# A graph transformer on one core: q fetched two quads in front, one bank for the maxima

## The chip, the cores and the metric

The kernel runs on one core of one Trainium2 chip. The metric is the device time of the whole program in microseconds, the median of the runs. Three runs of the kernel before gave 4218.53, 4223.54 and 4201.57 us.

## The reference

The model is a graph transformer with two layers on 6250 nodes of 128 features and 100000 edges that are sorted by their target node, followed by a projection, a residual and a normalisation. There are 32 edge types, 16 node types and 8 heads of 16. One layer, cut to what matters here:

```python
q = typed_linear(x, ntype, Wq)                    # per node
kT = einsum('nhd,htdo->nhto', k, Watt)            # per node and edge type
vT = einsum('nhd,htdo->nhto', v, Wmsg)
kw, m = kT[src, :, etype], vT[src, :, etype]      # one row per edge
a = einsum('ehd,ehd->eh', kw, q[dst]) * pri / SQRT_D
att = edge_softmax(a, dst, n)                     # segment max, exp, sum, per target
hag = segment_sum(m * att, dst)                   # per target node
h = layernorm(silu(typed_linear(hag, ntype, Wa)) * alpha + x * (1 - alpha))
```

## The kernel before, in words

Each layer has two stages. The first (`fused`) computes k, v and q of the nodes and writes a table to memory: for each source node and edge type one row of 256 floats, 128 of the key and 128 of the message. The second (`attend`), the stage that the change touches, goes over the edges.

The edges lie in slots: 26 blocks of 32 tiles, a tile of 128 edges whose targets lie in one tile of 128 nodes. Four tiles make a quad, so a block has 8 quads and a layer 208. The order of work is written out by hand: each engine has its own program, a loop over blocks with the 8 quads (q = 0 to 7) written out, six blocks in a turn of the hardware loop. Engines wait for one another by semaphores that count quads. What each does in its step t:

- POOL (L795) gathers the table rows of the edges of a quad into `rows` by four indirect DMAs of 128 rows of 1 KB. `rows` holds three blocks. Quad t+11 may be gathered when quad t-13 has been summed; in the first three blocks POOL is held by `q_psum` instead, ten quads ahead (`LEAD`).
- DVE builds the turned one-hot matrix of a quad (`turned`, L1752): it compares the edges' places in the node tile, loaded by SP into a ring of four, with the row number. A matrix has 128 x 512 floats and lies in `region_q` behind the q of all nodes. There are two places.
- PE fetches q of each edge by matmuls of this matrix with the q of the node tile (`fetch_q`, L1270), four matmuls (eight records in the profile) into bank 1 or 2. It does this for quad t+1.
- DVE multiplies the gathered keys by q from the bank (`multiply`, L1744), sums over each head (`head_sums`, L1757), and later weighs messages by the exponentials (`weigh`, L1766, quad t-12).
- PE sums the weighted messages and weights per node (`sum_quad`, L1283, quad t-13) with one-hot matrices that ACT builds (L1014, L1017), and DVE adds the four results to `sums` (`add`, L1781, quad t-14).
- The maxima of the block before are found by a chain that is spread over the steps q = 0 to 5 (`find_maxima`): DVE masks the scores, PE turns them (L1313, q = 0, bank 3), DVE scans (L1812, L1815), PE brings the chunk ends into a row (L1321, q = 1, bank 4), DVE carries them on (L1822 and below), PE turns them back (L1327, q = 2, bank 4), DVE adds them (L1838 to L1844), PE turns the maxima (L1334, q = 3, bank 3), DVE subtracts them (L1850), ACT takes the exponentials. In q = 5 PE spreads the factor of a node whose edges cross the block border (L1297, bank 4).

In a step PE has the order: crossing (q = 5), sum, fetch, chain step. DVE has the order: multiply, crossing (q = 6), then four places, each with one addition; behind the addition of place 0 the one-hot matrix of quad t+2, of place 1 the head sums, of place 3 the weighing; and behind these the chain's step of that place. The waits of the fetch and of its matrix are

```python
pe.wait_ge(onehotT_ready, quad + 1)
wait(pe, prod_ready, quad - 1)         # the multiplication that used the bank last
...
wait(dve, q_psum, quad - 1)            # the fetch that used the matrix's place last
```

At the end of the second layer POOL stores the sums by indirect DMAs (L805) while the last quads are still at work.

## Time and profile before

| | us |
|---|---|
| runs: median, lowest, highest | 4218.53, 4201.57, 4223.54 |
| profiled execution: span | 4190.3 |
| of that, attention of layer 0 (641 to 2010) | 1369 |
| of that, attention of layer 1 (2621 to 4010) | 1389 |
| DVE busy | 2714.8 (65%) |
| POOL busy | 2540.4 (61%) |
| PE busy | 2425.6 (58%) |
| ACT busy | 1707.4 (41%) |

The page gives the profiled execution a span, from the first to the last instruction, and no further time. Busy times are of the whole span. In the two attention stages the traffic is about 110 to 120 GB/s, in the stages that write the table about 400 GB/s. "Idle before" is the time in which an instruction's engine did nothing just before it, and the name behind it is what ended that. Ends of matmuls are modelled, not measured. "Remote" means that the view knows no instruction of this core that ended the wait.

### The profile page before, as it was taken

The numbers are of one execution on the slowest core, as the hardware profiler recorded it, in microseconds if no ns is written. First come the engines' busy times: TensorE is split into PE (matmuls) and PEld (weight loads), VectorE is DVE, ScalarE is ACT, GpSimd is POOL, SyncE is SP. The second block draws the span as 40 slices with busy tenths as digits, with TensorE's granted clock in tenths as the row PEclk, the third lists the DMA queues.
The fourth block names the chain that finished last, engine by engine and source line by source line (L and its number), as shares of the span: only waits on it lengthen the run. The fifth ranks groups of instructions, "written<-read, shape, count | busy, mean of one in ns | idle before, by whom it ended". The sixth has DMA issues, their size and how long they took to land.

```text
span 4190.3 us, 54460 instructions
## 1 busy us (share of the span) xinstructions
PE 2425.6 (58%) x12785; PEld 1767.6 (42%) x12786; DVE 2714.8 (65%) x6706; ACT 1707.4 (41%) x3970; POOL 2540.4 (61%) x2596
## 2 busy tenths in 40 slices
PE   3777771455555556556677777145555555555355
PEld 2333331355445555455333333144544444444343
DVE  7666662566666666667778877156766667666465
ACT  3666660233223333324566666022333333223255
POOL 4666556666666666661566664666666666666426
PEclk8899885677777777776799888577777777777666
DMA  8999984344444444444799997444444444444131
GB/s 202 406 412 409 417 356 136 110 118 123 123 117 117 120 119 120 116 115 109 249 382 375 409 390 326 131 114 117 116 114 113 113 113 112 114 113 114 51 112 48
DMA packets 321826, 782.64 MB, mean 187 GB/s; under 512 B 87083, under 2 KB 249803, under 8 KB 309007
## 3 DMA queue, kind: packets, MB, share of 16 engines
q0 software_dynamic: 110672, 651.37, 44.2%
q1 hardware_dynamic: 202387, 127.10, 11.7%
q8 instruction: 126, 2.06, 0.2%
q10 hardware_dynamic: 8448, 0.53, 0.1%
q14 instruction: 193, 1.58, 0.1%
HBM read 335.58 MB, written 573.46 MB: 217 GB/s over the span
## 4 chain that ended last, share of the span: by engine, by line
DVE 19%; issue 19%; PE 18%; DMA 16%; another core or an unknown queue 16%; ACT 5%; DVEq 4%; POOL 3%; SPq 0%; POOLq 0%; ACTq 0%
DMA relation_table<-region,scatter_node 14%; PE bank L1283 6%; DVE sums L1781 6%; PE bank L1270 4%; PE bank L1116 3%; ACT region L878 3%; DVE region L1766 2%; DVEq L1770 1%; DVE region L1744 1%; DVEq L1781 1%; DVE region_q L1752 1%; PE bank L1146 1%; PE bank L1321 1%; DVEq L396 1%
## 5 line engine op out<-in xcount | busy, mean ns | idle before, releaser
L795 POOL DMA_INDIRECT region<-relation_table,key_of x1664 | 1634.6, 982 | 886.5 <-issue 461.9
L1283 PE MATMUL bank<-region,arena 128*128 128x136 f32 x3328 | 694.3, 371 | 514.5 <-DVE region L1766 298.4
L1014 ACT ACTIVATE arena<-iota_free,minus_dst 128x128 f32<-128x128 f32 x1664 | 528.4, 388 | 831.7 <-remote 433.9
L1283 PEld LDWEIGHTS bank<-region,arena 128*128 128x128 f32 x3328 | 600.6, 262 | 594.6 <-DVE sums L1781 290.0
L1744 DVE TENSOR_TENSOR region<-bank,region 128x512 f32<-128x512 f32 x416 | 285.1, 685 | 871.2 <-remote 670.3
L1116 PE MATMUL bank<-sums,arena 128*128 128x512 bf16 x2048 | 630.7, 418 | 244.0 <-ACT region L878 212.2
L878 ACT COPY region<-bank 128x512 f32<-128x512 f32 x1152 | 624.4, 601 | 359.9 <-DMA relation_table<-region,scatter_node 220.9
L1570 DVE COPY region<-bank 128x512 f32<-128x512 f32 x896 | 585.5, 685 | 264.7 <-DMA relation_table<-region,scatter_node 173.5
L1270 PE MATMUL bank<-region_q 128*128 x3328 | 604.5, 342 | 187.9 <-issue 99.4
L1270 PEld LDWEIGHTS bank<-region_q 128*128 128x128 f32 x3328 | 570.8, 257 | 201.7 <-issue 201.2
L1781 DVE TENSOR_TENSOR sums<-sums,bank 128x136 f32 x1664 | 473.6, 285 | 78.7 <-DVE sums L1781 29.9
L1025 ACT ACTIVATE region<-arena 128x256 f32<-128x256 f32 x52 | 21.7, 417 | 1031.4 <-DVE arena L1850 789.2
L1116 PEld LDWEIGHTS bank<-sums,arena 128*128 128x128 bf16 x2048 | 197.0, 103 | 577.1 <-ACT region L878 295.8
L1766 DVE TENSOR_TENSOR region<-region 128x512 f32<-128x512 f32 x416 | 284.0, 683 | 2.1
L1757 DVE TENSOR_REDUCE arena<-region 128x32 f32<-128x512 f32 x416 | 280.4, 674 | 0.1
L1017 ACT ACTIVATE arena<-arena 128x512 f32<-128x512 f32 x416 | 262.0, 630 | 13.1
L718 POOL TENSOR_TENSOR sums<-arena,sums 128x256 f32<-128x256 f32 x128 | 86.1, 673 | 266.2 <-ACT arena L896 262.7
L1752 DVE TENSOR_SCALAR region_q<-arena,row_no 128x512 f32<-128x512 bf16 x416 | 206.9, 497 | 13.8 <-issue 7.3
L1577 DVE COPY arena<-bank 128x1024 bf16<-128x1024 bf16 x256 | 175.4, 685 | 49.9 <-issue 14.1
L1137 PE MATMUL bank<-identb,sums 128*128 128x128 bf16 x2048 | 176.2, 236 | 4.1 <-POOL sums L722 4.1
L1137 PEld LDWEIGHTS bank<-identb,sums 128*128 128x128 bf16 x2048 | 152.9, 107 | 58.5 <-issue 18.4
L735 POOL DMA_INDIRECT relation_table<-region,scatter_node x128 | 128.9, 1007 | 73.6 <-issue 33.3
(243 smaller groups left out, 2655.3 us busy)
## 6 DMA issues: line engine op xcount, KB each, us to landing
arena<-edge_places SPq DMA_DIRECT2D x416, 128.0 KB
region<-relation_table,key_of POOLq DMA_INDIRECT x1664
arena<-segment_flags SPq DMA_DIRECT2D x104, 128.0 KB
region_q<-q_rows SPq DMA_DIRECT2D x6, 768.0 KB, 6.5
aggregated_rows<-one_less_alpha SPq DMA_DIRECT2D x17, 256.0 KB
region<-aggregated_rows SPq DMA_DIRECT2D x16, 272.0 KB, 3.0
sums<-relation_weight_parts SPq DMA_DIRECT2D x32, 128.0 KB
x_sorted<-arena SPq DMA_DIRECT2D x16, 256.0 KB
```

The costliest lines, as they stand in the source:

```text
L795: pool.indirect_dma_start(out=rows[:, block_.r, q * QUAD + s], out_offset=None, in_=table, in_offset=bass.IndirectOffsetOnAxis(ap=key_of[: ...
L878: nc.scalar.copy(stage[:, r, :, k * HS:(k + 1) * HS], bank[TABLE_BANK + k % TABLE_BANKS][:, :].rearrange("p (t o) -> p t o", t=RT)).then_i ...
L1014: chain.step(nc.scalar.activation(onehots[:, at, s], iota_free[:, :], ACT.Abs, bias=minus_dst[:, bass.ds(block_.b * BLOCK + (q * QUAD + s) ...
L1116: nc.tensor.matmul(bank[TABLE_BANK + k % TABLE_BANKS][:, :], x_spreadT[:, k, :], w_rel[:, k, :], start=True, stop=True).then_inc(table_psu ...
L1137: ins = nc.tensor.transpose(bank[SPREAD_BANK[half]][:, :].bitcast(BF16)[:, k * P:(k + 1) * P], x_spread[:, tile.par, half * H + k].rearran ...
L1270: ins = nc.tensor.matmul(bank[1 + q % 2][:, s * D:(s + 1) * D], onehotT[:, q % 2, s], q_rows[:, bass.ds(tiles[s], 1), :].rearrange("p a n ...
L1283: ins = nc.tensor.matmul(bank[SUM_BANK[q % 2][pair]][:, s * SUMC:(s + 1) * SUMC], onehots[:, at, 2 * pair + s], rows[:, block_.r, slot, RH ...
L1570: v.tensor_copy(stage[:, r, :, k * HS:(k + 1) * HS], bank[TABLE_BANK + k % TABLE_BANKS][:, :].rearrange("p (t o) -> p t o", t=RT)).then_in ...
L1744: v.tensor_tensor(here, bank[1 + q % 2][:, :].rearrange("p (s d) -> p s d", s=QUAD), here, ALU.mult).then_inc(prod_ready, 1)
L1757: v.tensor_reduce(score[:, block_.par, q * QUAD:(q + 1) * QUAD, :], rows[:, block_.r, q * QUAD:(q + 1) * QUAD, 0:D].rearrange("p s (h o) - ...
L1766: v.tensor_tensor(msg, msg, bc(part[:, :, RHS0:D], 3, HS), ALU.mult).then_inc(weighted, 1)
L1781: v.tensor_tensor(total, total, bank[SUM_BANK[q % 2][n // 2]][:, (n % 2) * SUMC:(n % 2 + 1) * SUMC], ALU.add).then_inc(sum_added, 1)
```

## The change

q is fetched for quad t+2 in PE's step t, and its one-hot matrix is built for quad t+3 in DVE's step t. The q lies in banks 1, 2 and 4 in turn, the matrices in three places, and all five steps of the maxima on PE use bank 3. The place of a quad is its number in the layer modulo 3. In front of the first step PE fetches two quads instead of one, and DVE builds three matrices instead of two.

```diff
+Q_BANK = (1, 2, 4)
+Q_AHEAD = len(Q_BANK) - 1
+CHAIN_BANK = 3
...
-        onehotT = wqf[:, NTILES * D:NTILES * D + 2 * QUAD * P].rearrange("p (r s e) -> p r s e", r=2, s=QUAD)
+        onehotT = wqf[:, NTILES * D:NTILES * D + len(Q_BANK) * QUAD * P].rearrange("p (r s e) -> p r s e", r=len(Q_BANK), s=QUAD)
...
+        def q_place(block_, q):
+
+            return (block_.at * QPB + q) % len(Q_BANK)
+
...
                     pe.wait_ge(onehotT_ready, quad + 1)
-                    wait(pe, prod_ready, quad - 1)
+                    wait(pe, prod_ready, quad - Q_AHEAD)
+                    at = q_place(block_, q)
                     for s in range(QUAD):
-                        ins = nc.tensor.matmul(bank[1 + q % 2][:, s * D:(s + 1) * D], onehotT[:, q % 2, s],
+                        ins = nc.tensor.matmul(bank[Q_BANK[at]][:, s * D:(s + 1) * D], onehotT[:, at, s],
...
                         if q % 2 == 0:
-                            tiles = slot_tiles(block_.b, q + 1)
-                        coming = ahead(block_, q, 1)
+                            tiles = slot_tiles(block_.b, q + Q_AHEAD)
+                        coming = ahead(block_, q, Q_AHEAD)
...
-                fetch_q(Block(0, 0), 0, slot_tiles(0, 0))
+                tiles = slot_tiles(0, 0)
+                for q in range(Q_AHEAD):
+                    fetch_q(Block(0, 0), q, tiles[QUAD * q:])
...
-                    v.tensor_tensor(here, bank[1 + q % 2][:, :].rearrange("p (s d) -> p s d", s=QUAD), here, ALU.mult).then_inc(prod_ready, 1)
+                    v.tensor_tensor(here, bank[Q_BANK[q_place(block_, q)]][:, :].rearrange("p (s d) -> p s d", s=QUAD), here, ALU.mult).then_inc(prod_ready, 1)
...
-                    wait(dve, q_psum, quad - 1)
-                    flat = onehotT[:, q % 2].rearrange("p s e -> p (s e)")
+                    wait(dve, q_psum, quad - Q_AHEAD)
+                    flat = onehotT[:, q_place(block_, q)].rearrange("p s e -> p (s e)")
...
-                        coming = ahead(block_, q, 2)
+                        coming = ahead(block_, q, Q_AHEAD + 1)
...
-                for q in range(2):
+                for q in range(Q_AHEAD + 1):
                     turned(Block(0, 0), q)
```

Everywhere else `bank[3]` and `bank[4]` of the chain (L1297, L1313, L1321, L1327, L1334 on PE and their readers on DVE) become `bank[CHAIN_BANK]`.

## Rows read from the trace of the kernel before

**Rows 1.** Windows, attention stages: stretch, length, busy us by engine, clock, DMA share, GB/s.
```profile
641.00:2010.00 1369.00, 733.65 (x3818) 644.70 (x3819) 849.83 (x2321) 405.91 (x1104) 826.45 (x843) 0.71 0.44 118
2621.00:4010.00 1389.00, 702.81 (x3796) 611.82 (x3796) 834.75 (x2288) 402.20 (x1093) 858.89 (x874) 0.72 0.39 108
```

**Rows 2.** The chain that ended last, shares of the span by engine.
```profile
DVE 19%; issue 19%; PE 18%; DMA 16%; another core or an unknown queue 16%; ACT 5%; DVEq 4%; POOL 3%; SPq 0%; POOLq 0%; ACTq 0%
```

**Rows 3.** Groups of the page: busy us, mean ns, idle before and its main releaser.
```profile
L795 POOL DMA_INDIRECT region<-relation_table,key_of x1664 | 1634.6, 982 | 886.5 <-issue 461.9
...
L1744 DVE TENSOR_TENSOR region<-bank,region 128x512 f32<-128x512 f32 x416 | 285.1, 685 | 871.2 <-remote 670.3
...
L1270 PE MATMUL bank<-region_q 128*128 x3328 | 604.5, 342 | 187.9 <-issue 99.4
...
L1781 DVE TENSOR_TENSOR sums<-sums,bank 128x136 f32 x1664 | 473.6, 285 | 78.7 <-DVE sums L1781 29.9
...
L1752 DVE TENSOR_SCALAR region_q<-arena,row_no 128x512 f32<-128x512 bf16 x416 | 206.9, 497 | 13.8 <-issue 7.3
```

**Rows 4.** Line L1744: what ended the idle time before it, us and times.
```profile
  remote: 670.3, 130
  PE bank L1270: 117.5, 50
```

**Rows 5.** Timeline of 1438 to 1454 us: start, length, instruction, idle before.
```profile
1439.29 0.69 DVE L1744 TENSOR_TENSOR region<-bank,region 128x512 f32<-128x512 f32 x1 [2.68 <-remote]
...
1444.54 1.92 PE L1283 MATMUL bank<-region,arena 128*128 128x136 f32 x8 [0.39 <-issue]
...
1446.26 1.92 PE L1270 MATMUL bank<-region_q 128*128 x8
...
1446.69 0.95 POOL L795 DMA_INDIRECT region<-relation_table,key_of  x1 [0.30 <-PE bank L1283]
...
1447.97 0.53 PE L1334 MATMUL bank<-ident,arena 128*128 128x128 f32 x2
...
1452.07 0.69 DVE L1744 TENSOR_TENSOR region<-bank,region 128x512 f32<-128x512 f32 x1 [3.90 <-PE bank L1270]
```

**Rows 6.** Timeline of PE, 1426 to 1440 us.
```profile
1432.89 1.05 PE L1270 MATMUL bank<-region_q 128*128 x8
```

**Rows 7.** Windows: first burst of gathers, steady, without gathers, stores (columns as rows 1).
```profile
655.00:725.00 70.00, 7.79 (x32) 6.63 (x32) 7.06 (x14) 0.00 (x0) 50.60 (x54) 0.51 0.40 114
850.00:1890.00 1040.00, 599.20 (x3148) 528.20 (x3148) 689.88 (x1894) 331.20 (x902) 675.48 (x687) 0.74 0.44 119
1900.00:1950.00 50.00, 34.98 (x201) 30.02 (x200) 46.02 (x131) 21.51 (x58) 0.00 (x0) 0.81 0.34 94
3881.00:3937.00 56.00, 7.72 (x32) 7.19 (x32) 4.52 (x12) 3.81 (x10) 39.24 (x41) 0.51 0.17 57
```

**Rows 8.** Timeline of 720 to 742 us.
```profile
725.65 2.07 PE L1270 MATMUL bank<-region_q 128*128 x8 [20.23 <-issue]
...
736.98 0.69 DVE L1744 TENSOR_TENSOR region<-bank,region 128x512 f32<-128x512 f32 x1 [10.87 <-remote]
...
737.66 0.94 POOL L795 DMA_INDIRECT region<-relation_table,key_of  x1 [7.90 <-remote]
```

**Rows 9.** Line L795: what ended POOL's idle time before it, beside "issue".
```profile
  issue: 461.9, 1467
  remote: 253.1, 95
  PE bank L1283: 118.2, 76
  PE bank L1270: 42.0, 24
```

**Rows 10.** Waits, 850 to 1890 us: total, times, longest.
```profile
DVE region L1744 <- remote: 208.7, 59, 9.4
...
DVE region L1744 <- PE bank L1270: 58.4, 20, 6.0
```

**Rows 11.** Waits, 655 to 737 us.
```profile
DVE region L1744 <- remote: 52.2, 3, 20.7
```

More of the change, by code:

```diff
@@ L1296, in step @@
                         pe.wait_ge(cross_ready, turn_no)
-                        nc.tensor.matmul(bank[4][:, 0:H], cross_hot[:, :], lower[:, :], start=True, stop=True).then_inc(rescale_psum, 1)
+                        nc.tensor.matmul(bank[CHAIN_BANK][:, 0:H], cross_hot[:, :], lower[:, :], start=True, stop=True).then_inc(rescale_psum, 1)
                     late = late_quad(block_, q, FIRST_SUMMED)
@@ L1312, in step @@
                         for n in range(PER_CHUNK):
-                            ins = nc.tensor.transpose(bank[3][:, n * P:(n + 1) * P],
+                            ins = nc.tensor.transpose(bank[CHAIN_BANK][:, n * P:(n + 1) * P],
                                                       masked[:, n].rearrange("p j h -> p (j h)"), ident[:, :])
@@ L1320, in step @@
                         for n, column in enumerate((fwd[:, CLEN - 1:CLEN], first_seg[:, CLEN - 1:CLEN], bwd[:, 0:1], last_seg[:, 0:1])):
-                            ins = nc.tensor.matmul(bank[4][0:1, n * P:(n + 1) * P].rearrange("o (h j) -> o h j", h=H),
+                            ins = nc.tensor.matmul(bank[CHAIN_BANK][0:1, n * P:(n + 1) * P].rearrange("o (h j) -> o h j", h=H),
                                                    column, by_head, start=True, stop=True)
@@ L1326, in step @@
                         for n in range(2):
-                            ins = nc.tensor.matmul(bank[4][:, n:n + 1], carry_rows[0:1, n].rearrange("o j h -> o (j h)"),
+                            ins = nc.tensor.matmul(bank[CHAIN_BANK][:, n:n + 1], carry_rows[0:1, n].rearrange("o j h -> o (j h)"),
                                                    ones[0:1, 0:1], start=True, stop=True)
@@ L1333, in step @@
                         for n in range(PER_CHUNK):
[L1334 removed]
+                            ins = nc.tensor.transpose(bank[CHAIN_BANK][:, n * P:(n + 1) * P], edge_max[:, n * P:(n + 1) * P], ident[:, :])
                         ins.then_inc(max_T, 1)
@@ L1786, in scale_crossing @@
                     dve.wait_ge(rescale_psum, b + (l * NBLOCKS + 1))
-                    link(v.tensor_scalar(rescale[:, :], bank[4][:, 0:H], 1.0, None, ALU.add))
+                    link(v.tensor_scalar(rescale[:, :], bank[CHAIN_BANK][:, 0:H], 1.0, None, ALU.add))
                     wait(dve, sum_added, b * BLOCK + l * NQUADS * QUAD)
@@ L1811, in find_maxima @@
                         dve.wait_ge(masked_T, before + 1)
-                        chain.step(v.tensor_tensor_scan(fwd[:, :], flags[:, old, 0, :], bank[3][:, 0:CLEN], -BIG, ALU.add, ALU.max))
+                        chain.step(v.tensor_tensor_scan(fwd[:, :], flags[:, old, 0, :], bank[CHAIN_BANK][:, 0:CLEN], -BIG, ALU.add, ALU.max))
                     if (q, place) == (1, 1):
@@ L1818, in find_maxima @@
                         dve.wait_ge(chunk_rows, before + 1)
-                        got = bank[4][0:1, :].rearrange("o (k h j) -> o k h j", k=4, h=H)
+                        got = bank[CHAIN_BANK][0:1, :].rearrange("o (k h j) -> o k h j", k=4, h=H)
                         for n in range(2):
@@ L1837, in find_maxima @@
                         dve.wait_ge(carry_T, before + 1)
-                        chain.step(v.tensor_copy(chunk_carry[:, :], bank[4][:, 0:2]))
+                        chain.step(v.tensor_copy(chunk_carry[:, :], bank[CHAIN_BANK][:, 0:2]))
                     if (q, place) == (3, 1):
@@ L1850, in find_maxima @@
                         v.tensor_tensor(by_half(below_max[:, :, :]), masked[:, :],
-                                        bank[3][:, 0:CLEN].rearrange("p (i j h) -> p i j h", i=PER_CHUNK, h=H),
+                                        bank[CHAIN_BANK][:, 0:CLEN].rearrange("p (i j h) -> p i j h", i=PER_CHUNK, h=H),
                                         ALU.subtract).then_inc(below_ready, 1)
-                        chain.step(v.tensor_tensor(lower[:, :], carry_in[0:1, 0, 0, :, 0], bank[3][0:1, 0:H], ALU.subtract))
+                        chain.step(v.tensor_tensor(lower[:, :], carry_in[0:1, 0, 0, :, 0], bank[CHAIN_BANK][0:1, 0:H], ALU.subtract))
                         v.tensor_copy(carried[:, :], carry_out[0:1, 0, :, CHUNKS])
```

1 line of the change is left out of this document (removed).

## Prediction

> **What bounds the kernel now.** I read the time by stage first. The two attention stages, 641 to 2010 and 2621 to 4010 us, hold 1369 and 1389 of the 4190.3 us of the span, and only they are touched [rows 1]. No engine is full in them: DVE works 850 of 1369 us, POOL 826, PE 734. The chain that ended last gives 16% of the span to "another core or an unknown queue" and 18% to PE [rows 2]. The groups say where that lies: the multiplication by q (L1744) has 871.2 us of idle DVE time in front of it, while the 1664 additions of sums have 78.7 us [rows 3]. Of the 871.2 us, 670.3 in 130 waits end by "remote" and 117.5 in 50 waits by the q fetch L1270 [rows 4]. That instruction waits for two things only, its gathered rows and its q. The gathers are issued eleven quads ahead, so what it waits for is q from PE, also where the view has no name for it.
>
> The timeline shows the kind of wait. A sum starts at 1444.54 and the fetch behind it at 1446.26, recorded to end at 1448.18; the multiplication starts at 1452.07, 3.9 us later [rows 5]. Another quad's fetch, recorded at 1432.89 with 1.05 us [rows 6], is used at 1439.29 [rows 5]. So PE's results come 4 to 5 us after the end that the record gives. This happens while POOL issues gathers. Where POOL issues none (1900 to 1950) DVE is busy 46.0 of 50 us, against 690 of 1040 us in the steady stretch [rows 7]. Where POOL issues without a break it is worst: 54 gathers in 655 to 725 us beside 32 fetch matmuls, eight to a quad, so 17.5 us a quad; 41 DMAs in 3881 to 3937 beside two PE steps [rows 7]. And at 725.65 a fetch is recorded, POOL then falls silent for 7.9 us, and the multiplication starts only at 736.98 [rows 8]. I call this the late result.
>
> The loop is closed: POOL gathers quad t+11 when PE has summed quad t-13, PE sums it when DVE has weighed it one step before, DVE cannot weigh while it waits for q. A quad takes 1040/(687/4) = 6.05 us in the steady stretch [rows 7]. POOL's own work is 4 gathers of 0.982 us and 0.31 us between them [rows 3, 9], 5.2 us, and its waits besides "issue" are 253.1 + 118.2 + 42.0 = 413 us of the run [rows 9]. That is the most that the loop can give before POOL alone is the bound.
>
> **The change part by part.** Nothing is added or taken from the work of a quad: the same 8 fetch matmul records (0.342 us), the same one-hot comparison (0.497 us), multiplication (0.685 us) and additions (0.285 us) [rows 3], in the same places of each engine's order. Only the number of the quad moves: in step t PE fetches q for t+2 instead of t+1, and DVE builds the one-hot matrix of t+3 instead of t+2. The waits come out at the same events: PE's fetch still waits for the multiplication of t-1 (three banks, one quad more ahead), DVE's comparison still for the fetch of t, which the multiplication in front of it has waited for. The load of edge places still has four steps. Across a block it is held by the scans instead of the ring, at most one step later, with some 20 us left. The price of these is 0. In the prologue there is one more fetch and one more comparison per layer, 8 x 0.342 and 0.5 us, beside a gather of 5.2 us: 0 to 3 us each layer, taken as 0.
>
> The one bank for five chain steps: each step's PE write already waits for the DVE instruction behind the reading of the previous one (scans, carries, maxima, the crossing), so no new order arises. Price 0. If a step did have to wait for one more DVE instruction of the size of the multiplication, that would be 52 blocks x 4 x 0.685 = 142 us at most, but no wait in the code could do that.
>
> Now the gain. With the change the multiplication of t needs a fetch that PE did two steps before. A late result of 4 to 5 us is within one DVE step. So the 3.9 us at 1452.07 vanish there. What is late next depends on the step of the block:
> - q = 1 to 4. The chain step waits for a PE result that stands behind the late fetch in PE's order (the two transposes at 1447.97 [rows 5]). DVE gets in front of it the multiplication, one addition and the comparison, 0.685 + 0.285 + 0.497 = 1.47 us; the rest of the wait moves there.
> - q = 0, 5, 6, 7. The first addition needs the sum of PE's last step, which stands in front of the fetch. If only the fetch is late, the wait goes whole; if the sum is late too, DVE gains the 0.685 us of the multiplication.
>
> The steady stretch of the first layer has 208.7 + 58.4 us in 59 + 20 waits, 3.4 us each [rows 10]; the stretch has 172 quads, both layers 376 without their starts and ends, so 584 us in 173 waits. Lower end if late results stay as they are: 173 x 0.685 = 119 us. Upper end: half the waits at 1.47 us, half whole, 87 x 1.47 + 86 x 3.4 = 420 us, cut to the 413 us that POOL has. The lower end is nearer to what I expect, because the late results answer to POOL: a POOL that waits less issues longer without a break. Of the 119 us I leave a quarter to that, by choice, and take 119 x 0.75 = 90 us. With the whole feedback the gain is 0, and below 0 in the third rival.
>
> The waits outside the steady stretch I cost at 0. Before block 3 and in the stores at the end, PE has the next fetch in its queue already and delivers one in 17 to 28 us; a deeper queue brings nothing. POOL's own limit there, ten quads ahead of the fetches, moves one quad: 5.2 us either way.
>
> The Trainium skill (SBUF — State Buffer, Who interferes with whom) says that only the port pair of VectorE and GpSimd is shared and that PE waits for nobody at SBUF. The rows speak against it as far as time goes: PE's results are late just where POOL issues. By that rule a busier POOL could do PE no harm, my quarter would fall away, and the sum would be 119 us, 4099 us.
>
> **Sum.** 4190.3 - 90 = 4100 us of span. The page gives no other time of its execution; the runs' median of 4218.5 us lies 28.2 us above the span, which I take as what lies around it. Forecast 4128 us.
>
> **The rivals.**
> 1. The wait only changes its place. If PE, not its latency, is slow beside POOL, each result is late by PE's work and the additions and chain steps take over all of the wait. For it: the 17.5 us a quad, with the next fetch long queued [rows 7]. Against it: at 1446 the sum just ahead was on time by its record and released the gather at 1446.69, while the fetch alone was late [rows 5]. Also here: that the lookahead does not arise because PE's place in the loop is the same. 4218 us, within 10.
> 2. The waits go nearly whole: 300 of the 413 us. For it: additions have only 78.7 us of idle time in front of 1664 of them [rows 3]. Against it: half the steps have the chain behind, and the feedback. 3918 us.
> 3. Slower: POOL, less held up, issues in longer unbroken rows, and PE falls into the state of 655 to 725 us. A wait of 3.4 us becomes up to 20.7 us there [rows 11], 17.3 us more. 119/17.3 = 7 of the 173 waits turn the sign. With 12 it is 208 - 119 = 89 us slower, 4307 us. For it: the state exists. Against it: in the steady part a gather needs a sum, so POOL stops by itself when PE falls behind, and the waits there are 9.4 us at most [rows 10].
>
> **How the numbers follow.** Forecast 0.45, rival 1 0.25, rival 2 0.15, rival 3 0.15. The forecast's own range is 4070 to 4180 us. The range that should hold 8 in 10 reaches from 3980 (half of rival 2 inside, near the 119 us doubled) to 4240 (rival 1 whole): rival 3 and the far part of rival 2 are left out. A measurement here can tell about 0.5%, 21 us, from no change. Faster by more: the forecast nearly whole, rival 2, together 0.59 and a little of rival 1: 0.61. Within: 0.23. Slower: rival 3 and a tail of rival 1: 0.16.
>
> **What would show it.** Idle time before L1744 falls from 871 us to under 350, apart from the starts and the stores, where it stays at about 20 us a wait. Idle time before the additions and before the chain's readers L1812, L1822, L1838, L1850 rises by 200 to 400 us. POOL's waits fall by about 90 us, and are fewer and longer apart. If the chain's readers and the additions take all of it, rival 1 is right; if DVE's waits of over 15 us appear in the steady stretch, rival 3. I am wrong in the mechanism if the waits before L1744 stay: then it was not q that it waited for.

## The result, and the profile after

The kernel with the change takes 4193.88 us (median of 7 runs, 4189.25 to 4198.36), the kernel before 4218.53 us (7 runs, 4201.57 to 4226.09): ratio 0.9947, 95% interval 0.9934 to 0.996. It is 25 us faster; 90 were forecast. The time lies inside the range that should hold 8 in 10 (3980 to 4240 us) and outside the forecast's own (4070 to 4180 us). The profiled execution of after has a span of 4191.9 us and its runs lie 2 us above such spans. That of before, with 4190.3 us, was quicker than any of its timed runs, so the two traces, laid side by side, show no gain at all; where the time is, they show.

The groups of the page after (columns as in [rows 3]):

```profile
L802 POOL DMA_INDIRECT region<-relation_table,key_of x1664 | 1630.7, 980 | 899.9 <-issue 467.5
...
L1278 PE MATMUL bank<-region_q 128*128 x3328 | 589.5, 328 | 313.1 <-issue 225.2
...
L1791 DVE TENSOR_TENSOR sums<-sums,bank 128x136 f32 x1664 | 474.0, 285 | 281.8 <-remote 181.0
...
L1754 DVE TENSOR_TENSOR region<-bank,region 128x512 f32<-128x512 f32 x416 | 283.6, 682 | 291.4 <-remote 257.2
...
L1848 DVE COPY chunk_carry<-bank 128x2 f32<-128x2 f32 x52 | 8.2, 157 | 337.9 <-remote 337.9
...
L1762 DVE TENSOR_SCALAR region_q<-arena,row_no 128x512 f32<-128x512 bf16 x416 | 203.8, 490 | 13.8 <-issue 13.6
```

The idle time before the multiplication (now L1754) fell from 871.2 to 291.4 us. The additions (L1791) took over 203 of the 580 us, from 78.7 to 281.8, and one chain reader (L1848, the copy of the carries) has 337.9 us in front of it, where it had 29.4 us as L1838. Multiplication, additions and the chain's four readers of PE's bank together have 1028 us of idle time before them in the kernel before and 1012 us now. POOL's idle time is 899.9 us, where it had 886.5 [rows 3]. The windows of the same stretches say the same of the engines:

```profile
655.00:725.00 70.00, 7.36 (x32) 6.31 (x32) 6.46 (x12) 0.00 (x0) 50.21 (x53) 0.52 0.40 109
850.00:1890.00 1040.00, 555.81 (x3110) 474.51 (x3110) 680.71 (x1871) 325.28 (x887) 668.66 (x681) 0.76 0.43 118
1900.00:1950.00 50.00, 33.52 (x194) 29.00 (x193) 44.76 (x124) 26.92 (x73) 1.64 (x2) 0.83 0.34 88
3881.00:3937.00 56.00, 7.25 (x32) 6.01 (x32) 4.33 (x12) 2.54 (x6) 41.15 (x42) 0.55 0.18 59
```

681 gathers in 1040 us are 6.11 us a quad, against 687 and 6.05 [rows 7]. The first burst and the stores look as before. The timeline shows how PE's results come out, 1428 to 1435 us of after:

```profile
1428.66 2.18 PE L1291 MATMUL bank<-region,arena 128*128 128x136 f32 x8 [3.90 <-issue]
...
1430.08 0.94 POOL L802 DMA_INDIRECT region<-relation_table,key_of  x1 [0.30 <-issue]
...
1430.63 1.48 PE L1278 MATMUL bank<-region_q 128*128 x5
...
1433.15 0.69 DVE L1754 TENSOR_TENSOR region<-bank,region 128x512 f32<-128x512 f32 x1 [4.13 <-remote]
1433.17 0.57 PE L1278 MATMUL bank<-region_q 128*128 x3 [1.06 <-issue]
1433.45 1.28 ACT L1021 ACTIVATE arena<-iota_free,minus_dst 128x128 f32<-128x128 f32 x4 [11.25 <-remote]
...
1434.13 1.13 POOL L802 DMA_INDIRECT region<-relation_table,key_of  x1 [3.11 <-PE bank L1278]
```

POOL's last issue ends at 1431.02. PE's fetch stands still in the middle of its group, five matmuls and then three. At 1433.15, 2.1 us after POOL fell silent, VectorE, PE and ScalarE all go on within 0.3 us, and POOL itself starts a microsecond later. VectorE and ScalarE go on with results that PE's record had long finished. POOL stops because its own gate is a fetch of PE; here it is the one that stood still.

How general this is, the same trace tells. Of VectorE's 55 waits of over 1.5 us between quads 30 and 182 of the first layer, 42 end while POOL is silent, 2.1 us after the end of its last record by the median; the other 13 end while POOL issues. The trace also has the time of each packet and of each semaphore signal. From the start of a gather's issue to the end of its last packet, counted off in order, it takes 2.4 to 2.7 us by the median and never over 4.5 us, in the unbroken row at a layer's start as in the steady stretch. So the rows are not behind; what is late is the signal of PE's results. PE makes 416 fetches, and the trace of after holds 386 of their signals, so it misses some; the next one behind a fetch's recorded end comes 4.1 us later by the median.

### The profile page after: what moved, and what is told of

It reads as the page before. It is cut to its first block, busy times and chain, and to the rows that moved or that the text cites. A ratio compares the mean times of both kernels' runs of the same rounds, so it can differ in the third digit from the quotient of the medians.

```text
span 4191.9 us, 54366 instructions
## 1 busy us (share of the span) xinstructions
PE 2356.6 (56%) x12695; PEld 1692.8 (40%) x12786; DVE 2714.6 (65%) x6706; ACT 1704.9 (41%) x3970; POOL 2537.3 (61%) x2596
## 4 chain that ended last, share of the span: by engine, by line
DVE 17%; another core or an unknown queue 14%; issue 11%; DMA 8%; PE 6%; DVEq 4%; POOL 3%; ACT 1%; SPq 0%; POOLq 0%; ACTq 0%
DMA relation_table<-region,scatter_node 7%; DVE sums L1791 5%; PE bank L1291 2%; DVE region L1754 2%; DVEq L1780 2%; PE bank L1123 1%; DVEq L1791 1%; PE bank L1278 1%; DVE region L1776 1%; DVE region_q L1762 1%; POOL region_q L709 1%; DVE region L1580 1%; ACT region L885 1%; DVEq L403 1%
## 5 line engine op out<-in xcount | busy, mean ns | idle before, releaser
L802 POOL DMA_INDIRECT region<-relation_table,key_of x1664 | 1630.7, 980 | 899.9 <-issue 467.5
L1291 PE MATMUL bank<-region,arena 128*128 128x136 f32 x3328 | 657.1, 356 | 366.0 <-issue 136.5
L1278 PE MATMUL bank<-region_q 128*128 x3328 | 589.5, 328 | 313.1 <-issue 225.2
L1123 PE MATMUL bank<-sums,arena 128*128 128x512 bf16 x1958 | 609.0, 418 | 257.2 <-ACT region L885 178.0
L1291 PEld LDWEIGHTS bank<-region,arena 128*128 128x128 f32 x3328 | 564.3, 248 | 457.5 <-issue 286.0
L1278 PEld LDWEIGHTS bank<-region_q 128*128 128x128 f32 x3328 | 540.3, 242 | 319.6 <-issue 318.4
L1791 DVE TENSOR_TENSOR sums<-sums,bank 128x136 f32 x1664 | 474.0, 285 | 281.8 <-remote 181.0
L1754 DVE TENSOR_TENSOR region<-bank,region 128x512 f32<-128x512 f32 x416 | 283.6, 682 | 291.4 <-remote 257.2
L1342 PE MATMUL bank<-ident,arena 128*128 128x128 f32 x104 | 34.3, 431 | 385.0 <-DVE arena L1854 384.2
L1848 DVE COPY chunk_carry<-bank 128x2 f32<-128x2 f32 x52 | 8.2, 157 | 337.9 <-remote 337.9
L1329 PE MATMUL bank<-ident,arena 128*1 128x128 f32 x416 | 104.7, 409 | 192.8 <-DVE arena L1825 185.3
```

What stands on the lines that cost most here:

```text
L802: pool.indirect_dma_start(out=rows[:, block_.r, q * QUAD + s], out_offset=None, in_=table, in_offset=bass.IndirectOffsetOnAxis(ap=key_of[: ...
L1123: nc.tensor.matmul(bank[TABLE_BANK + k % TABLE_BANKS][:, :], x_spreadT[:, k, :], w_rel[:, k, :], start=True, stop=True).then_inc(table_psu ...
L1278: ins = nc.tensor.matmul(bank[Q_BANK[at]][:, s * D:(s + 1) * D], onehotT[:, at, s], q_rows[:, bass.ds(tiles[s], 1), :].rearrange("p a n -> ...
L1291: ins = nc.tensor.matmul(bank[SUM_BANK[q % 2][pair]][:, s * SUMC:(s + 1) * SUMC], onehots[:, at, 2 * pair + s], rows[:, block_.r, slot, RH ...
L1754: v.tensor_tensor(here, bank[Q_BANK[q_place(block_, q)]][:, :].rearrange("p (s d) -> p s d", s=QUAD), here, ALU.mult).then_inc(prod_ready, 1)
L1791: v.tensor_tensor(total, total, bank[SUM_BANK[q % 2][n // 2]][:, (n % 2) * SUMC:(n % 2 + 1) * SUMC], ALU.add).then_inc(sum_added, 1)
```

## The experiments

Two notes for reading them. On the first occasion (the first four runs) the kernel before took 3716 us in place of 4218; what differs there I could not find. Ratios are always against before on the same occasion, and a difference in us between kernels of two occasions is good to some 5 us. "A quad" is the time of four gathers in the steady stretch: 950 us divided by a quarter of the gathers that the POOL group of 900 to 1850 us counts.

**First occasion: before takes 3716.47 us (25 runs).** Each of these four changes one thing of the changed kernel.

```diff
-Q_BANK = (1, 2, 4)
+Q_BANK = (1, 2)
```

> One part of the change alone: all five chain steps in one bank, q still one quad ahead in two banks. By every theory this changes no wait: within 0.3% of the kernel before (4218 us), its idle time before the multiplication as before, about 870 us. If the shared bank costs something, it is slower by more than 20 us.

Measured 3716.17 us, ratio 1.0 (0.999 to 1.0009).

```diff
-                    for s in range(QUAD):
-                        pool.indirect_dma_start(out=rows[...], in_=table, in_offset=...)
...
+                        sp.dma_start(rows[:, b % DEPTH, q * QUAD + s], table[first:first + P, :])
```

> The kernel after with the gather changed: the rows of a quad come by four plain DMAs from SP's queue (the next 128 rows of the table instead of the edges' own rows, same bytes), POOL issues none of them. Theory A (PE's results are signalled late while POOL issues indirect DMAs): PE's results come within 0.5 us of their recorded ends, idle time before the multiplication, the additions and the reader of the carries together falls from 911 us to under 100, a quad falls from 6.1 to about 4.4 us (DVE's own work), the run to about 4194 - 376 x 1.7 = 3550 us. Theory B (PE's own work is slow beside any traffic into SBUF, whoever issues it): the waits stay, the run stays within 100 us of 4194.

Measured 3253.63 us, ratio 0.8754 (0.8736 to 0.8773).

```diff
-pool.indirect_dma_start(out=rows[:, block_.r, q * QUAD + s], out_offset=None, in_=table,
+pool.indirect_dma_start(out=rows[:, block_.r, q * QUAD + s, 0:D], out_offset=None, in_=table.rearrange("n (k d) -> (n k) d", k=2),
```

> The kernel after with half rows: POOL gathers 512 bytes instead of 1 KB for each edge (other rows of the table, the message half of the rows is left as it was), with the same number of indirect DMAs and rows. Theory A (late by POOL's issuing): no change, 4150 to 4200 us, waits as in the kernel after. Theory C (late by the bytes that the gathers move): the waits fall by about half, the run by 200 us or more.

Measured 3707.41 us, ratio 0.9976 (0.9966 to 0.9987).

```diff
-nc.tensor.matmul(bank[Q_BANK[at]][:, s * D:(s + 1) * D], onehotT[:, at, s], ...)
+nc.tensor.matmul(bank[Q_BANK[at]][:, s * D:s * D + D // 2], onehotT[:, at, s], ...)
```

> The kernel after with half the fetch: PE fetches 64 of the 128 floats of q for each edge and the multiplication reads them twice, so PE has about 0.7 us less work in a quad and DVE the same. Theory A (results are held, not computed slowly): waits nearly as in the kernel after, within 40 us of 4194. Rival (PE's own rate beside POOL is the limit, the first rival of the prediction): PE delivers a quad in clearly less time, 0.5 us or more of a quad, 150 to 250 us faster.

Measured 3714.6 us, ratio 0.9989 (0.9978 to 0.9999).

The groups of the first of them, with q one quad in front:

```profile
L802 POOL DMA_INDIRECT region<-relation_table,key_of x1664 | 1646.8, 990 | 517.7 <-issue 483.8
...
L1754 DVE TENSOR_TENSOR region<-bank,region 128x512 f32<-128x512 f32 x416 | 287.0, 690 | 460.6 <-DMA region<-relation_table,key_of 446.4
```

On this occasion POOL waits for next to nothing (517.7 us idle, 483.8 of it the gaps between issues), the multiplication waits for gathered rows, and no result of PE is late: each of the 416 signals of its fetches comes 0.01 us behind the recorded end. 581 gathers in 750 us are 5.16 us a quad, four times 0.99 and 0.31: POOL's issue is the bound. Half the bytes or half the fetch can change little there and save 9 and 2 us, so these two runs do not separate their theories. Half the bytes are tried again below; half the fetch is not. Without POOL's gathers the kernel is 463 us faster. The shared bank costs nothing.

**Second occasion: before takes 4215.38 us (11 runs).** The condition of the first measurement is back.

No edit, the changed kernel itself:

> The whole change, unaltered, beside the kernel before on the same chip. Theory A (the change shortens only waits for results of PE that come late while POOL issues gathers, and where these results are on time POOL's issue of the gathers, 4 x (0.99 + 0.31) = 5.2 us a quad, is the bound): where the kernel before takes about 3716 us, ratio 1.000 within 0.002, idle before the multiplication about 460 us and ended by the gathered rows, POOL waiting for almost nothing; where the kernel before takes about 4218 us, ratio 0.995 as in the first measurement. Theory B (the gain comes from having q's sums earlier, whatever holds them up, or from the bank shared by the maxima's steps): ratio about 0.994 in either case.

Measured 4195.75 us, ratio 0.9945 (0.9927 to 0.9962): the 0.5% repeat.

```diff
-LEAD = 10
+LEAD = 4
```

> The change with LEAD = 4: POOL may issue the gathers of quad t once the fetch of q for quad t - 4 is done, instead of t - 10, so POOL runs at most four quads in front. Theory A (POOL's issue is the bound and its lead over the loop is not needed beyond the landing of the rows, about 2.5 us after issue): 3716 within 0.5% where the kernel before takes 3716; where it takes 4218, POOL stops more often for PE's result, every unbroken row of gathers is shorter, a held result is let out sooner, and the start of each layer (188 us for 24 quads) falls to 5 us a quad plus one wait of 4 us each 4 quads, about 150 us: 4194 - 2 x 35 = 4120. Theory B (what POOL issues in front is what keeps the rows in time): each of some 6 waits of POOL's own adds its length to the bound engine, and the time rises by 1 to 3%.

Measured 4148.65 us, ratio 0.9844 (0.9826 to 0.9862).

```diff
                 for c in range(FIRST_LATE):
+                    if c % 2 == 0:
+                        pool.wait_ge(sum_added, 4 * (l * NQUADS + NQUADS - 22 + c // 2))
                     store_sums(c)
```

> The change with the 22 early stores of sums at the end of a layer put behind sums that are complete one after another (each pair waits for the next quad's adds), where now POOL issues them in one unbroken row. Theory A (an unbroken row of POOL's issues holds back PE's results, 40 us without a multiplication at the end of layer 2 in the profile): where the kernel before takes 4218, 2 x 30 us less than 4194, so about 4130; where it takes 3716, PE's results are on time under any row, and the time is the same within 0.3%. Theory B (the 40 us at the end are the gathers that POOL has not issued yet): no difference in either case, or up to 20 us more because the stores end later.

Measured 4145.76 us, ratio 0.9837 (0.9815 to 0.9859).

Both take 47 to 50 us more (74 and 64 were expected), and both at the edges: with LEAD = 4 the first 24 quads of the two layers take 157 and 161 us in place of 187 and 186, and the moved stores shorten the end of layer 2. POOL's group of the steady stretch, 900 to 1850 us, first of after, then with LEAD = 4:

```profile
L802 POOL DMA_INDIRECT region<-relation_table,key_of x623 | 611.6, 982 | 339.7 <-issue 174.7 <-remote 80.0 <-PE bank L1278 63.0
```

```profile
L802 POOL DMA_INDIRECT region<-relation_table,key_of x628 | 614.4, 978 | 338.2 <-issue 334.6 <-PE bank L1291 3.7
```

6.10 and 6.05 us a quad, with the same idle time of POOL, 340 and 338 us, although its lead is less than half. That was the hint: what I had called waits that the loop could give did not depend on POOL's lead.

**Third occasion: before takes 4223.85 us (7 runs).**

LEAD = 4 and the stores together:

> The change with both of the last two edits: LEAD = 4, and the stores at the end of a layer put behind sums that are complete. Both shortened a stretch outside the steady one (LEAD = 4 the two starts, 187 to 157 and 186 to 161 us for 24 quads; the stores the end of layer 2, 91 to 37 us). Theory A (the stretches are separate): the gains add up, 4216 x (0.9945 - 0.0101 - 0.0108) = 4216 x 0.9736 = 4105. Theory B (time saved in a start is given back in the steady stretch, since one path that POOL's issue goes through sets the whole): at most the larger of the two, about 4145. Where the kernel before takes 3716 on this occasion: the same within 0.3%.

Measured 4118.74 us, ratio 0.9754 (0.9736 to 0.9773): 77 us less than after, where the two edits alone took 97 together. By the ratios it is 1.9 of 2.1%, and theory A's 0.9736 is the edge of the interval: they add up, or nearly. It is the fastest of all the kernels here that compute the reference.

```diff
-                        dve.wait_ge(carry_T, before + 1)
-                        chain.step(v.tensor_copy(chunk_carry[:, :], bank[CHAIN_BANK][:, 0:2]))
+                        dve.wait_ge(scans_ready, before + 1)
+                        chain.step(v.tensor_copy(chunk_carry[:, :], bwd[:, 0:2]))
...
+                        for done in (masked_T, chunk_rows, carry_T, max_T):
+                            wait(dve, done, before)
```

(and the same for the other readers of the chain's bank but the rescaling; the maxima are left out of this kernel's result)

> The four readers of the maxima's steps on VectorE read SBUF in place of PE's bank and wait for signals of VectorE itself; PE still does its steps (the maxima are left out of the result). In the kernel after, VectorE waited 338 us before the reader of the carries alone. Theory A (the waits of the chain's readers took the place of the wait before the multiplication, and set the rate now): the steady stretch falls from 6.10 to at most 5.5 us a quad, so 4195 - 350 x 0.6 = 3985 or less. Theory B (the rate is POOL's: 5.07 us of issue and 1.04 us of stops a quad, the same in the kernels before, after, with LEAD = 4 and with the stores moved, and any wait of VectorE only shows it): 6.1 us a quad as before, total within 1% of 4195, and the idle time goes to the adds and the multiplication. Where the kernel before takes 3716 on this occasion: 3716 within 0.5%, by both.

Measured 4187.04 us, ratio 0.9914 (0.9891 to 0.9937). Its groups:

```profile
L802 POOL DMA_INDIRECT region<-relation_table,key_of x1664 | 1641.5, 986 | 882.0 <-issue 460.4 <-remote 206.5 <-PE bank L1278 121.5
L1791 DVE TENSOR_TENSOR sums<-sums,bank 128x136 f32 x1664 | 472.5, 284 | 525.3 <-remote 323.6 <-issue 122.2 <-DVE sums L1791 30.1
L1754 DVE TENSOR_TENSOR region<-bank,region 128x512 f32<-128x512 f32 x416 | 283.1, 681 | 473.4 <-remote 353.6 <-issue 93.2 <-PE bank L1278 26.2
```

The chain's waits are gone, and the additions and the multiplication have 525.3 and 473.4 us in their place. Together they are 999 us, against 1012 for the additions, the multiplication and the chain's readers of after. VectorE's idle time goes wherever the next reader of PE stands; its sum is set elsewhere.

```diff
                     for s in range(QUAD):
                         pool.indirect_dma_start(...).then_inc(rows_in[block_.r][q], 16)
+                    wait(pool, paced, block_.quad(l, q) - 1)
+                    nc.gpsimd.tensor_tensor(pace[:, q % 2], ones[:, 0:GROUP], minus_half[:, 0], ALU.pow).then_inc(paced, 1)
```

> After the four gathers of each quad POOL does one small operation of its own (a power of 128x4 values, 1.05 us in the trace of before) that has nothing to do with the rest. Theory A (PE's results are held while POOL issues and are let out only when it has stopped, and each stop costs its time): 4 x 1.29 + 1.05 + stops of 1.04 = 7.2 us a quad, 350 x 1.05 = 370 us slower, about 4560. Theory B (the path behind POOL's issue takes some 6.1 us a quad, POOL's rows of issues of 5.1 us a quad run ahead of it and the stops only let it catch up): a pace of 6.2 us of POOL's own leaves nothing to catch up, PE's results are on time, the stops vanish, and the time is within 1.5% of 4195 in spite of 437 us more work on POOL; the starts fall from 187 to about 150 us for 24 quads, so 4130 may come out. Where the kernel before takes 3716 on this occasion, POOL's issue is the bound and it is slower by 416 x 1.1 = 450 us: 4170.

Measured 4170.3 us, ratio 0.9874 (0.9853 to 0.9895). POOL has 461 us more work and the kernel is 25 us faster than after on the second occasion (0.7% by the ratios). Its groups of POOL and of the multiplication:

```profile
L804 POOL DMA_INDIRECT region<-relation_table,key_of x1664 | 1648.5, 991 | 469.6 <-issue 447.1 <-DMA relation_table<-region,scatter_node 11.3 <-PE bank L1295 10.5
...
L808 POOL TENSOR_TENSOR pace<-ones,minus_half 128x4 f32<-128x4 f32 x416 | 461.0, 1108 | 10.1
L1758 DVE TENSOR_TENSOR region<-bank,region 128x512 f32<-128x512 f32 x416 | 287.7, 692 | 881.3 <-DMA region<-relation_table,key_of 843.2 <-PE bank L1282 31.8 <-issue 5.9
```

POOL now waits for next to nothing. The 432 us in which it waited beyond its gaps in after (899.9 - 467.5) are filled by 461 us of useless work, the steady rate is 6.19 us a quad (614 gathers in 950 us), and the multiplication waits for rows, as on the first occasion, and hardly for PE. The first 24 quads of a layer take 148 us by the multiplications' starts in place of 188. So the gain is at the edges: the two starts are 79 us shorter, while quads 24 to 191 of the two layers take 29 us longer together.

The gathers as plain transfers by SyncE, once more:

> The rows are fetched by plain transfers that SyncE issues (contiguous rows, so the result is another), POOL issues nothing in the attention stage: the same kernel that took 3254 us where the kernel before took 3716. Theory A and B (what holds PE's results is POOL's issue of the gathers, and only that): 3254 within 1% on this occasion too, even where the kernel before takes 4216; idle before the multiplication below 20 us. Theory C (in that condition PE's results are late whoever issues the transfers, or VectorE, PE or the DMA engines are slower): the time stays above 3600.

Measured 3297.56 us (one run), 1.3% over 3254 where 1% was allowed. Without POOL's gathers the two occasions are 44 us apart, 3254 and 3298; with them 490 to 507 us. Idle before the multiplication:

```profile
L1759 DVE TENSOR_TENSOR region<-bank,region 128x512 f32<-128x512 f32 x416 | 281.8, 678 | 8.3 <-issue 8.2
```

The transfers differ from the gathers in two ways, in who issues them and in that their rows lie one behind another, and by themselves these runs do not tell the two apart. But POOL is not quite silent in this kernel: at the end of layer 2 it stores the sums by a row of 42 indirect DMAs. The same 70 us from the start of that row, now and on the first occasion, and the longest wait of VectorE in them now:

```profile
2970.00:3040.00 70.00, 22.50 (x112) 19.61 (x112) 24.00 (x70) 10.35 (x30) 41.75 (x42) 0.59 0.31 100
2973.00:3043.00 70.00, 49.57 (x292) 42.25 (x292) 65.58 (x185) 32.59 (x89) 42.94 (x42) 0.83 0.47 146
DVE chunk_carry L1853 <- issue: 20.1, 1, 20.1
```

POOL does the same work in both, 42 to 43 us. Beside it VectorE is busy 24.0 us now and 65.6 us on the first occasion, and these 42 us are nearly the whole difference of 44 us between the two runs. Of the 416 signals of PE's fetches 413 come within 0.01 us of the recorded end; the other three, 16 to 47 us late, fall into this row. So in one and the same run PE's results are on time while SyncE moves the rows and late while POOL issues, and stores do it as gathers do.

**Fourth occasion: before takes 4220.57 us (7 runs).**

The gathers of 512 B once more:

> The gathers fetch 512 B of each row instead of 1056 B, as many transfers of as many rows as before (the results use stale halves). Theory A (the 6.1 us a quad are time for bytes): the stops of POOL, 1.04 us a quad, go, 5.2 us a quad, about 4195 - 350 x 0.9 = 3880 or less. Theory B (they are time for transfers or rows, or come from the way in which PE's results are held while POOL issues, whatever the size): 6.1 us a quad, 4195 within 0.7%. Where the kernel before takes 3716 on this occasion: 3707 as in the first run.

Measured 4197.69 us, ratio 0.9944 (0.9925 to 0.9964), 6.10 us a quad: not bytes. (A row has 1024 B, 256 floats; the 1056 B of the expectation are a slip.)

```diff
-                    nc.gpsimd.tensor_tensor(pace[:, q % 2], ones[:, 0:GROUP], minus_half[:, 0], ALU.pow).then_inc(paced, 1)
+                    nc.gpsimd.memset(pace[:, q % 2], 0.0).then_inc(paced, 1)
```

> Like e11_paced, but POOL's own small operation after each quad's gathers is a memset of 128x4 values (0.1 to 0.2 us in the trace of before) instead of the power of 1.05 us. Theory A (any break in the issue of gathers lets PE's held results out, however short): POOL runs without a stop at 4 x 1.29 + 0.2 = 5.3 to 5.4 us a quad, about 4170 - 370 x 0.85 = 3855. Theory B (a path behind POOL's issue takes some 6.1 us for a quad, or a break must last as long as it takes to catch up, about 1 us a quad): the stops are back, 6.1 us a quad, the starts are 187 us again, 4195 within 0.7%. Where the kernel before takes 3716 on this occasion: slower than it by 416 x 0.15 = 60 us.

Measured 4199.09 us, ratio 0.9948 (0.9928 to 0.9968). POOL's groups of 900 to 1850 us:

```profile
L804 POOL DMA_INDIRECT region<-relation_table,key_of x621 | 611.0, 984 | 320.5 <-issue 163.4 <-remote 75.6 <-PE bank L1282 60.1
L808 POOL MEMSET pace<- 128x4 f32 x156 | 19.1, 122 | 0.1
```

A break of 0.12 us lets nothing out: the stops are back, 6.12 us a quad. They are shorter by just what the memsets take, 339.7 - 320.5 = 19.2 us beside 19.1.

The paced kernel with the moved stores:

> e11_paced (1.05 us of other work on POOL after each quad's gathers) with the stores at the end of a layer put behind complete sums. Theory A (the end of layer 2 is a stretch of its own, in which an unbroken row of stores holds PE's results): the end of e11_paced took 57 us for the last ten quads, e5 brought that of after from 91 to 37, so 20 us less than 4170: 4150. Theory B (pacing has taken that gain already): 4170 within 0.2%.

Measured 4149.9 us, ratio 0.9833 (0.9817 to 0.985), as theory A said. But the moved stores alone gave 0.9837: beside them the pace brings nothing.

The kernel before, paced in the same way:

> The kernel before (q one quad in front) with the same pace. In e11_paced POOL is the bound at 6.2 us a quad and PE's fetch of q still comes 3.3 us late by the median. Theory A (q two quads in front is what makes this lateness harmless): with one quad in front each fetch has one step less of cover, the multiplication waits for PE on part of the quads and the loop is slower than POOL's 6.2 us: 4200 to 4300. Theory B (cover of one step, 4 to 6 us, is enough for results that are at most one row of four gathers late): 4170 within 0.5%, and the change is worth nothing beside a paced POOL.

Measured 4167.63 us, ratio 0.9873 (0.9854 to 0.9893). q one quad in front is enough beside a paced POOL; the change is worth nothing there.

**Fifth occasion: before takes 4215.41 us (21 runs).**

```diff
-pool.indirect_dma_start(out=rows[:, block_.r, ...], in_offset=...(ap=key_of[:, ...]))
+pool.indirect_dma_start(out=rows[0:P // 2, block_.r, ...], in_offset=...(ap=key_of[0:P // 2, ...]))
```

> The change with gathers of 64 rows each in place of 128, in as many transfers (half of the partitions keep stale rows). Theory A (the 6.1 us of four gathers go with rows): the path takes 3.1 us a quad, POOL never has to stop, the steady rate falls to VectorE's own or POOL's issue, at most 5.2 us a quad: 3880 or less. Theory B (they go with transfers): 6.1 us a quad and 4195 within 0.7%. Where the kernel before takes 3716 on this occasion, only POOL's own issue time tells something: at most 3716.

Measured 4202.14 us, ratio 0.9965 (0.9955 to 0.9976). POOL's group of 900 to 1850 us:

```profile
L802 POOL DMA_INDIRECT region<-relation_table,key_of x622 | 587.6, 945 | 361.3 <-issue 182.7 <-remote 86.8 <-PE bank L1278 55.5
```

Half the rows shorten the issue by 4% (945 against 982 ns), and the stops grow by as much: 6.11 us a quad. It does not go with rows. That it goes with the number of transfers is what is left; no run changed that number.

The change without its third bank, once more:

> The change without its main part: the maxima's steps share one bank, q is fetched one quad in front as before, in two banks. Theory A (the measured 0.5% is the fetch two quads in front, in the starts and ends and not in the steady stretch): ratio 1.000 within 0.002, starts as in before, 193 and 188 us for 24 quads. Theory B (the gain comes from another part, or from anything that shifts the kernel's steps): 0.995. The profile should be nearer the median than that of before was, and show the steady stretch of a typical execution: 6.1 us a quad by theory A.

Measured 4212.49 us (11 runs), ratio 1.0003 (0.9992 to 1.0015). The 0.5% are the fetch two quads in front, with the third bank and the third matrix that it needs, and not the shared bank. Its profiled execution, 4207.7 us, is a typical one of q one quad in front:

```profile
L802 POOL DMA_INDIRECT region<-relation_table,key_of x620 | 607.0, 979 | 344.8 <-issue 172.4 <-remote 113.5 <-PE bank L1291 36.7
L1754 DVE TENSOR_TENSOR region<-bank,region 128x512 f32<-128x512 f32 x416 | 284.7, 684 | 872.7 <-remote 659.0
L1848 DVE COPY chunk_carry<-bank 128x2 f32<-128x2 f32 x52 | 7.7, 148 | 22.7 <-remote 21.1 <-issue 1.4
```

(the first line of the window of 900 to 1850 us, the others of the whole run)

620 gathers in 950 us, 6.13 us a quad, against 6.10 for after. By the starts of the multiplications its two steady stretches (quads 24 to 199 and 232 to 399) take 1074.3 and 1030.4 us, and those of the changed kernel on the second occasion 1069.8 and 1019.6; the two starts differ by 6 us together. That is 21 us; the ends give 9 of them back, and the two spans, 4207.7 and 4195.4 us, differ by 12. As far as one execution each can tell, the gain, which I had looked for at the edges, is mostly in the steady stretch.

The kernel before with LEAD = 4 and the moved stores:

> The kernel before (q one quad in front, two banks for the maxima's steps) with LEAD = 4 and the stores put behind complete sums, the two edits of e8_both. Theory A (the steady rate is the path's 6.1 us, and q two quads in front helps only where POOL's rows of issues are long): with short rows the change is worth nothing: 0.9754 as e8_both within 0.002, 4119. Theory B (the change's 0.5% adds to the other two): 0.9754 + 0.0055 = 0.981, 4140.

Measured 4140.16 us, ratio 0.9817 (0.9802 to 0.9832), where the same edits on the changed kernel gave 0.9754: the change adds its 0.6% to them, as theory B said.

## Why the prediction was right or wrong

**What bounds the kernel: half right.** That PE's results come late where POOL issues gathers held. POOL's indirect DMAs are the cause: without the gathers the idle time before the multiplication is 8.3 us, and what is late in that run is late beside POOL's stores. But the loop that is only slow because DVE waits was wrong. In every unpaced kernel of this condition four gathers take 6.05 to 6.15 us in the steady stretch, with q one or two quads in front, LEAD 10 or 4, the chain read or not, 1024 or 512 B, 128 or 64 rows. POOL's record shows 5.2 us of this as issue and the rest as waits for PE.

**The price of the shared bank: right**, 0 (ratio 1.0 and 1.0003 without the third bank). A price of the new order cannot be told apart from its gain; it is not over it.

**The wait before the multiplication: right.** Forecast under 350 us from 871, measured 291.4. The starts stayed as they were (188 and 186 us for 24 quads, against 193 and 188). In the stores the longest wait before the multiplication is 21.0 us, against 33.7 before, but the additions wait beside it, 11.0 us at most.

**What is late next: right in place, wrong in size.** The additions and the chain's readers were to rise by 200 to 400 us. Against the typical kernel with one quad in front the additions rose by 205 us (from 77.2) and the four chain readers by 336 (from 103.7 to 439.3), 315 of them at L1848: 541 us, where the multiplication lost 581. By the prediction's own sign ("take all of it") this is rival 1. POOL's waits, which were to fall by about 90 us, stayed: 886.5 us of idle time before the gathers in before, 912.9 in the typical kernel, 899.9 in after.

**The failed step is the sum**: "173 x 0.685 = 119 us" as the lower end, and an upper end cut to "the 413 us that POOL has". It took what DVE gains at one place for time that the loop gains, and POOL's waits for time that the loop could give back. Neither is so. DVE's idle time at the readers of PE nearly stays: 1028 us in before (1054 in the typical kernel with one quad in front), 1012 in after and 999 without the chain's reads. POOL's waits stay as well, whatever its lead; a shorter issue makes them longer (the 64 rows), and work put into them costs the loop little: with 461 us of it four gathers take 6.19 in place of 6.10 us. In place of 90 us stand some 0.04 us a quad, 15 us over the 342 steady quads compared, and some 6 in the starts. Rival 1, "the wait only changes its place" (4218 within 10, chance 0.25), describes the mechanism and not the size, 25 us. Its argument, PE's own work as the cause, does not hold: with SyncE's transfers PE does the same work in 4.1 us a quad (quads 24 to 191 of the first layer in 690 us).

**The feedback**, my quarter for a POOL that issues longer rows, has the right sign: in the steady stretch the changed kernel stops less often and longer. From the gaps of over 0.8 us between POOL's issues, quads 30 to 182: 58 of 2.73 us, against 73 of 2.37 us with one quad in front. That this is what ate the gain is not shown: with LEAD = 4 there are 65 stops, and their sum is the same, 161 us against 159.

**The base**: "28.2 us lie around the span" was wrong. Spans lie 2 us below the runs; the profiled execution of before was some 26 us quicker than its median. From the median the forecast would have been 4218 - 90 = 4128 all the same.

**The rule weighed in the prediction** (the Trainium skill, SBUF — State Buffer, Who interferes with whom: only the port pair of VectorE and GpSimd is shared) is not refuted for SBUF's ports, but it doesn't cover this case: with half of the bytes, or half of the rows, PE's results are as late. Another page bears on it: the Trainium skill (Perfetto Trace Analysis, DMA Instruction — SWDGE (GPSIMD)) says that the recorded end of such an instruction is the end of writing its descriptors, not the end of its transfer. The trace agrees: POOL's record ends at 1431.02, the last packet of that gather at 1432.48. Everybody goes on at 1433.15, 0.7 us behind that packet; over the 42 waits that end while POOL is silent it is 0.65 us by the median. Why PE's results wait for it, neither the page nor a run says.

**Open.** What takes 6.1 us for four of POOL's transfers, and why it holds PE's results meanwhile, no trace here names. A path of fixed time for each transfer fits the steady rates to 2%, but it is not the moving of the rows, whose packets end within 4.5 us of the issue; and it does not explain why an unbroken row costs more than its share (188 us for the first 24 quads, 148 when paced). Breaks between 0.12 and 1.1 us were not tried, nor another number of transfers a quad, nor half the fetch in this condition. And why the same kernel took 3716 us on the first occasion, with 5.16 us a quad and no late result, stays open. The first and the second occasion were on the same chip, and in the kernel without its third bank, run in both conditions, the records' lengths agree within 3% (a gather 990 and 982 ns, a fetch matmul 352 and 342, a multiplication 690 and 684).

## What to carry to other kernels

Before a wait is priced, see whether it moves. If the idle time of the readers keeps its sum when one of them no longer waits (1012 and 999 us here), or if the waits of the "idle" producer stay the same to 1% when its lead is cut to less than half, the rate is set elsewhere, and the producer's waits are not there to be had. Filling the suspected engine's idle time with useless work is a cheap further test, to be read with care, since an engine with true slack bears it too. Here it told more: with 461 us of such work POOL waited for nobody, VectorE waited for POOL's rows and no longer for PE, and the kernel was 25 us faster. Where GpSimd issues indirect DMAs back to back, keep its rows short at the edges of the loop (a small lead, stores spread over the last quads): 77 us here, against 20 to 25 for one more bank.

## What the hardware showed that I had not expected

- An indirect DMA issued by POOL takes 1.53 us of the loop (6.1 us for four) whatever it moves: 128 rows of 1024 B, 128 of 512 B, or 64 rows; its record shows 0.98 us (0.95 with 64 rows) and 0.31 us between two, and in after its last packet ends 2.4 to 2.7 us after the start of the issue by the median, in an unbroken row too.
- While POOL issues, results of PE are held. PE itself stopped here in the middle of a group, and most waits end together about 2 us after POOL's last issue (1431.02, 1433.15; 42 of 55 waits); up to 21.0 us in an unbroken row. Stores by POOL do it as gathers do: VectorE was busy 24.0 of 70 us beside a row of 42, against 65.6 beside the same row on the first occasion.
- Both are a condition and not a property: on one of six occasions, that of the first measurement counted, the same kernel took 3716 us, with no late result and 1.29 us a transfer.
